# Mixture-of-experts layer on one Trainium2 core: the fourth unit of the shared expert's first row pair by seven products

## The chip, the cores and the metric

The kernel runs on one core of one Trainium2 chip. The metric is the device time of one execution in microseconds (us). Inside the core five engines run their own instruction streams and wait for each other by semaphores: TensorE (PE: matmuls, and PEld: loading their stationary operand), VectorE (DVE), ScalarE (ACT), GpSimd (POOL) and SyncE (SP), whose queue starts the transfers.

## The reference, cut to what matters

```python
# x: (8, 512, 256); gate, up: (256, 1024); down: (1024, 256); 8 experts, top 2 for each of the 8 rows
def _gemma_mlp(x, gate_w, up_w, down_w):
    g = einsum('bsh,hi->bsi', x, gate_w)
    u = einsum('bsh,hi->bsi', x, up_w)
    return einsum('bsi,ih->bsh', gelu(g) * u, down_w)
...
rw = softmax(router_logits); w, sel = top_k(rw, 2)          # weights of the two experts of a row
out = sum over the two experts of w * _gemma_mlp(x, skill_gate[e], skill_up[e], skill_down[e])
out = out + _gemma_mlp(x, shared_gate, shared_up, shared_down)
x = x + out
x = x + (x @ W_base.T + b_base + 2 * sum_e cond_8[e] * (x @ A_e.T) @ B_e.T)
```

## The kernel before, in words

All matmuls are fp32 in three passes. Each operand is split into a rounded part (hi, made on ACT by `take_hi`) and the rest (lo, made on DVE by `take_lo`, L1395, which reads the operand and its hi), and a product is hi x hi, hi x lo, lo x hi: three matmuls of 128x512 (`product`, L733). So nothing can be multiplied before ACT and then DVE have gone over it.

The shared expert comes first. The 8 rows are taken as four pairs (q = 0 to 3), the inner width of 1024 as four pieces of 256 (j = 0 to 3): unit u = 4q + j, 16 units (`NU`). A unit multiplies a 2x2 block matrix of weights (A11, A12, A21, A22; one each for gate and up) with a 2x2 block matrix of tokens (B11, B12, B21, B22). Units of q = 0 do it in the plain way: `outputs(u, GATE)` and `outputs(u, UP)`, four outputs each, two products an output, 24 matmuls. Units of q > 0 do it Strassen-Winograd's way: `matrix(u, part)`, seven products, 21 matmuls. For these, sums of weights (S1 to S4) and of tokens (T1 to T4) are needed: POOL makes them (`left_sums(j)`, four subtractions of 2x128 columns; the T sums at L633 to L647, of 512 columns), ACT and DVE split them (`split_sums`, `split_right`). They are made during q = 0 for q = 1, and the weight sums are kept.

The products land in four PSUM banks (`ring`). In the plain way ACT takes each gate output with GELU (`gelu_block`) and DVE multiplies it with the up output (`mul_block`, L1438, into `post`, semaphore `sh_mul`); ACT and DVE then split the result (`inner_part`), and TensorE multiplies it with the down weights (`shared_down_part`, 12 matmuls at a time). The order on TensorE for each unit is: gate of u, first half of down of u-1, up of u, second half of down of u-1. Output t of the gate of unit u waits until `mul_block` t of unit u-1 has emptied its bank, and output t of the up part until GELU t has emptied it. In `matrix`, products 0 to 3 open the four banks in turn, after three matmuls each in place of six.

Each engine's list is written out by hand, in the order of the program; an instruction that waits holds up all behind it. Around the change lie, for DVE, `turn_x` (STREAM_TRANSPOSE of the next rows' tokens, L1425), `route` (MAX and MAX_INDEX over the logits, L1491 to L1497), `route_weights` (nine small operations, L1502 to L1522), `split_left` (lo of the weights), `split_shared_down` and `split_right`; for ACT, an Exp for the routing (L1210), which needs another activation table than GELU, `take_xt` (copies of the turned tokens of q = 0) and the hi parts of the same splits.

Of the kernel before, what the change touches and what calls it, by code (L numbers as in the profile page):

```python
# [17 lines left out]
GATE, UP = 0, 1  # L18
# [17 lines left out]
def cond_resid_kernel(nc, x, cond, skill_gate, skill_up, skill_down, shared_gate, shared_up,  # L36
# [11 lines left out]
    NU = Q * PAIRS  # L48
    assert HC == 2 and TT == 4 and E * R == P and H == 256 and S == 512 and E == 8
# [15 lines left out]
    with ExitStack() as ctx:  # L65
# [93 lines left out]
        u1, v57 = (post[:, n * S:(n + 1) * S] for n in range(2))  # L159
        g_t = [post[:, (3 + n) * S:(4 + n) * S] for n in range(4)]  # L160
# [182 lines left out]
        t_made = sem("t_made")  # L343
        v_done = sem("v_done")
# [20 lines left out]
        def matrix_no(u, part):  # L365
            return 2 * (u - PAIRS) + part

        def products(u, part, n):
            return 8 * PAIRS + NP * matrix_no(u, part) + n + 1
# [7 lines left out]
        LEFT_SUMS = [5, 7, 9, 10]  # L377
# [21 lines left out]
        def _(sp):  # L399
# [92 lines left out]
            for q in range(Q - 1):  # L492
# [12 lines left out]
                if q == 1:  # L505

                    sp.wait_ge(experts_known, 1)
                    sp.wait_ge(left_ready, LEFT_SUMS[PAIRS - 1])
# [30 lines left out]
            def row(b, first, last):  # L539
                if first:  # L540
# [7 lines left out]
                    sp.wait_ge(c_done, 4 * (NU - PAIRS))  # L548
                    sp.wait_ge(c22_done, 2 * (NU - PAIRS))
# [36 lines left out]
        def _(pool):  # L586
# [6 lines left out]
            def left_sums(j):  # L593
# [4 lines left out]
                s1, s2, s3, s4 = (s_tmp[:, :, n, :] for n in (S1, S2, S3, S4))  # L598
# [10 lines left out]
            left_sums(0)  # L609

# [12 lines left out]
            for u in range(NU):  # L623
                q, j = divmod(u, PAIRS)
                qn = q + 1
                if q > 0:
                    c22(u, GATE)
                if qn < Q and j == 1:
# [11 lines left out]
                if q > 0:  # L640
                    c22(u, UP)
                if qn < Q and j == 1:

                    pool.wait_ge(xt_in, 4 * q + 4)
                    G.tensor_tensor(t_b, xt(1, 1), xt(1, 0), ALU.subtract).then_inc(t_made, 1)
                    pool.wait_ge(t_made, 4 * q + 1)
                    G.tensor_tensor(t_c, xt(1, 1), t_a, ALU.subtract).then_inc(t_made, 1)  # L647
                if u < PAIRS - 1:
# [79 lines left out]
        def _(pe):  # L728
# [63 lines left out]
            def matrix(u, part):  # L792
                q, j = divmod(u, PAIRS)
                m = matrix_no(u, part)
                if part == GATE and q == 1:
                    pe.wait_ge(left_ready, LEFT_SUMS[j])
                for n, (bank, a, b, opens) in enumerate(PRODUCTS):
# [21 lines left out]
                    else:  # L819
                        pe.wait_ge(v_done, m + 1)  # L820
                    product(ring[bank][:], [left(j, hl, part, a) for hl in range(2)],
                            [right(q, hl, b) for hl in range(2)], opens, True, not opens)\
# [36 lines left out]
            for u in range(1, NU):  # L859
                if u < PAIRS:  # L860
# [132 lines left out]
            def row(b, par, first):  # L993
                pe.wait_ge(x_ready, b + 1)
                for k in range(K):
# [20 lines left out]
                    else:  # L1016
                        pe.wait_ge(u1_done, 2 * (NU - PAIRS))
# [5 lines left out]
                    else:  # L1023
                        pe.wait_ge(c_done, 4 * (NU - PAIRS) - 1 + k)
# [35 lines left out]
        def _(act):  # L1060
# [6 lines left out]
            def split_left(j):  # L1067
                act.wait_ge(sh_landed[j], 32)
                take_hi(lefts(j, 0, slice(0, 2), S1, A12 + 1), raw4(j)).then_inc(left_hi, 1)

            def split_sums(j):

                act.wait_ge(s_made, j + 1)
                act.wait_ge(product_done, 8 * (j + 1))
                take_hi(lefts(j, 0, slice(0, 2), S2, S1 + 1), s_tmp).then_inc(left_hi, 1)
# [11 lines left out]
            def split_right(qn, n, src):  # L1087
                if qn > 0 and n == B11:

                    if qn > 1:  # L1090
                        act.wait_ge(product_done, products(PAIRS * (qn - 1) - 1, UP, NP - 1)
                                    if qn > 2 else 8 * PAIRS)
# [34 lines left out]
            def copy_out(u, part):  # L1127

                m = matrix_no(u, part)
                for n, to, bank in ((0, u1, 0), (1, v57, 2)):  # L1130
                    act.wait_ge(product_done, products(u, part, n))
                    if n == 0 and m > 0:

                        act.wait_ge(c_done, 2 * m)
                        act.wait_ge(c22_done, m)
                    nc.scalar.copy(to, ring[bank][:]).then_inc(copied, 1)
# [52 lines left out]
            for u in range(1, NU):  # L1189
# [3 lines left out]
                if q == 0:  # L1193
                    inner_part(u - 1, 2)
                    inner_part(u - 1, 3)
                    for t in range(4):
                        gelu_block(u, t, BANKS[t])
                    if u < PAIRS - 1:
                        split_left(u + 1)
# [8 lines left out]
                if u == 2:  # L1208
# [600 lines left out]
```

## Time and profile before

| | us |
|---|---|
| median of 3 runs | 804.69 (803.77 to 805.49) |
| the profiled execution | 805.0 |
| its span in the profile | 803.2 |
| TensorE busy | 795.5 (99%) |
| VectorE busy | 670.9 (84%) |
| ScalarE busy | 472.1 (59%) |
| GpSimd busy | 271.9 (34%) |

The profile's times count from the start of its span; the execution's own time is 1.8 us longer than the span. An engine is busy while an instruction of it runs; matmuls overlap, so that a busy TensorE says only that it had no gap.

### The profile page before, as it was taken

To read this page: it belongs to the slowest core of one execution; us is meant where nothing else is said; L and a number is where in the kernel's file an instruction comes from. 1 tells how busy PE (TensorE), PEld (TensorE's weight loads), DVE (VectorE), ACT (ScalarE), POOL (GpSimd) and SP (SyncE) were. 2 spreads that over 40 slices of the span, in tenths; PEclk is the share of its full clock that TensorE was granted. 3 is DMA by queue.
4 is the path that set the end of the run, shared out by engine and by line. 5 is a ranking of instruction groups with operands and counts; after the bars stand their busy time and mean duration, and the time that the engine had idled before them with its cause. 6 is when DMAs were issued, how large, how long until landed. Compare 5 with 4: busy or idle time off the path is not lost.

```text
span 803.2 us, 13016 instructions
## 1 busy us (share of the span) xinstructions
PE 795.5 (99%) x4014; PEld 679.7 (85%) x4014; DVE 670.9 (84%) x874; ACT 472.1 (59%) x715; POOL 271.9 (34%) x266
## 2 busy tenths in 40 slices
PE   9999999999999999999999999999999999999998
PEld 7888888888888888889888888888888888888887
DVE  3886987987876799799979879987987997999786
ACT  5574564564654565566556556656665665665563
POOL 1440321321110562443246044333404614423420
PEclk9999999999999999999999999999999999999999
DMA  6340520303213432353443335335244423634200
GB/s 198 86 119 11 147 79 12 120 1 97 100 40 80 159 117 79 105 144 107 137 122 97 104 101 158 111 104 131 89 125 138 122 79 104 161 97 135 66 1 28
DMA packets 120143, 80.56 MB, mean 100 GB/s; under 512 B 62481, under 2 KB 115473, under 8 KB 120081
## 3 DMA queue, kind: packets, MB, share of 16 engines
q1 hardware_dynamic: 120080, 79.88, 33.8%
q8 instruction: 21, 0.34, 0.2%
q14 instruction: 42, 0.34, 0.1%
HBM read 67.28 MB, written 12.58 MB: 99 GB/s over the span
## 4 chain that ended last, share of the span: by engine, by line
PE 91%; DVE 4%; issue 2%; POOL 1%; ACT 1%; DMA 0%; DVEq 0%; POOLq 0%; ACTq 0%
PE ps_ring L733 57%; PE ps_acc L733 33%; DVE inner_lo L1395 1%; DVE wide L1395 1%; DVE xc L1395 1%; PE ps_ring L853 1%; DVE post L1711 0%; DMA sh_scratch<-stage 0%; DVE post L1660 0%; PE ps_acc L941 0%; PE ps_acc L847 0%; ACT xc L1062 0%; DVE post L1651 0%; POOL post L692 0%; ACT wide L1062 0%
## 5 line engine op out<-in xcount | busy, mean ns | idle before, releaser
L733 PE MATMUL ps_ring<-xc,wide 128*128 128x512 f32 (+1 forms) x2076 | 454.9, 367 | 1.8 <-DVE post L1660 1.8
L733 PEld LDWEIGHTS ps_ring<-xc,wide 128*128 128x128 f32 x2076 | 366.1, 188 | 68.6 <-DVE post L1660 2.7
L1062 ACT CAST inner_hi<-post 128x512 fp32r<-128x512 f32 x192 | 117.8, 621 | 131.6 <-DVE post L1711 57.8
L733 PE MATMUL ps_acc<-inner_hi,wide 128*128 128x512 f32 x504 | 172.0, 390 | 0.0
L1395 DVE TENSOR_TENSOR inner_lo<-post,inner_hi 128x512 fp32r<-128x512 f32 x192 | 163.6, 866 | 6.7 <-ACT inner_hi L1062 5.7
L1065 ACT ACTIVATE post<-ps_ring 128x512 f32<-128x512 f32 (+1 forms) x132 | 73.4, 559 | 92.2 <-PE ps_ring L733 86.3
L733 PEld LDWEIGHTS ps_acc<-inner_hi,wide 128*128 128x128 f32 x504 | 94.7, 188 | 19.2
L692 POOL TENSOR_TENSOR post<-post 128x256 f32<-128x256 f32 x48 | 34.5, 740 | 214.6 <-DVE post L1662 214.6
L733 PE MATMUL ps_acc<-inner_lo,wide 128*128 128x512 f32 x252 | 98.3, 390 | 0.0
L1711 DVE SCALAR_TENSOR_TENSOR post<-post,coef_now,ps_ring 128x512 f32<-128x512 f32 x80 | 59.5, 744 | 42.1 <-PE ps_ring L733 39.0
L733 PE MATMUL ps_acc<-inner_hi,sh_dn 128*128 128x512 f32 x256 | 83.8, 389 | 0.0
L733 PE MATMUL ps_ring<-xc 128*128 128x256 f32 x576 | 77.2, 283 | 0.5 <-DVE post L1711 0.5
L621 POOL TENSOR_TENSOR post<-post 128x512 f32<-128x512 f32 x24 | 31.1, 1294 | 135.5 <-DVE post L1447 135.5
L1395 DVE TENSOR_TENSOR wide<-raw,wide 128x1536 fp32r<-128x1536 f32 (+3 forms) x38 | 62.5, 1644 | 15.8 <-ACT wide L1062 15.8
L1065 ACT ACTIVATE post<-post 128x256 f32<-128x256 f32 (+1 forms) x84 | 46.4, 569 | 49.5 <-DVE post L1669 33.6
L733 PEld LDWEIGHTS ps_ring<-xc 128*128 128x128 f32 x576 | 72.6, 192 | 0.7 <-DVE post L1711 0.7
L1395 DVE TENSOR_TENSOR wide<-xbuf,wide 128x1536 fp32r<-128x1536 f32 x32 | 57.4, 1793 | 0.0
L733 PEld LDWEIGHTS ps_acc<-inner_hi,sh_dn 128*128 128x128 f32 x256 | 48.0, 188 | 9.9
L1062 ACT CAST wide<-raw 128x1536 fp32r<-128x1536 f32 (+3 forms) x40 | 52.2, 1306 | 4.8 <-DMA raw<-_L_cond_shared_gate_dram 3.7
L733 PEld LDWEIGHTS ps_acc<-inner_lo,wide 128*128 128x128 f32 x252 | 47.4, 188 | 9.0
L733 PE MATMUL ps_acc<-inner_lo,sh_dn 128*128 128x512 f32 x128 | 49.8, 389 | 0.0
L1395 DVE TENSOR_TENSOR xc<-stage,xc 128x1024 fp32r<-128x1024 f32 (+1 forms) x41 | 47.6, 1166 | 0.0
(122 smaller groups left out, 847.1 us busy)
## 6 DMA issues: line engine op xcount, KB each, us to landing
raw<-n_L_cond_skill_gate_dram SPq DMA_DIRECT2D x32, 256.0 KB, 2.9
raw<-in_L_cond_skill_up_dram SPq DMA_DIRECT2D x32, 256.0 KB, 3.4
raw<-n_L_cond_skill_down_dram SPq DMA_DIRECT2D x32, 256.0 KB, 3.7
xbuf<-n_L_cond_skill_gate_dram SPq DMA_DIRECT2D x32, 256.0 KB, 2.9
xbuf<-in_L_cond_skill_up_dram SPq DMA_DIRECT2D x32, 256.0 KB, 3.4
xbuf<-n_L_cond_skill_down_dram SPq DMA_DIRECT2D x32, 256.0 KB, 4.1
xt_scratch<-xbuf SPq DMA_DIRECT2D x8, 512.0 KB, 3.1
sh_scratch<-stage SPq DMA_DIRECT2D x8, 512.0 KB, 2.7
```

The source lines that it names most:

```text
L621: G.tensor_tensor((g_t if part == GATE else i_t)[3], v57, u1, ALU.add).then_inc(c22_done, 1)
L692: last = G.tensor_tensor(ex_v[:, half], ex_v[:, half], ex_u1[:, half], ALU.add)
L733: last = pe.matmul(dst, left_[a], right_[b], start=start and n == 0, stop=stop and n == len(PASSES) - 1, skip_group_check=adds)
L853: pe.transpose(ring[3][:, 0:P], ident[:], ident[:])
L1062: return nc.scalar.copy(dst, src)
L1065: return nc.scalar.activation(dst, src, ACT.Gelu_apprx_tanh)
L1395: return V.tensor_tensor(dst, src, hi.bitcast(F32), ALU.subtract)
L1711: V.scalar_tensor_tensor(out=inner[k % 2], in0=gelu[k % 2], scalar=coef_now[:, par, s:s + 1], in1=ring[2 + k % 2][:], op0=ALU.mult, op1=AL ...
```

## The change

The fourth unit (u = 3, j = 3 of q = 0) is computed by `matrix` too, 2 x 21 matmuls in place of 2 x 24. What that needs is made earlier:

- the four token sums of q = 0: POOL makes them behind `left_sums(0)`, ACT and DVE split them in the first unit (`split_first`), into buffers of q = 1 and q = 0 that are free then. For POOL to start, ACT copies the turned tokens before `split_left(1)`;
- the weight sums of j = 3: `left_sums(3)` and `split_sums(3)` move into the third unit (u = 2); they were made in the fourth, and split on ACT there and on DVE in the fifth;
- `route` moves on DVE from unit 2 to unit 1, `route_weights` from unit 3 to unit 2, and the Exp on ACT from behind the GELUs of unit 2 to ahead of them;
- T4 of q = 1, whose buffer the first sum uses, is split in unit 3, behind `sums(3, UP)`; `split_shared_down(3)` moves to the end of unit 3 on DVE; the hi part of the weights of j = 3 leaves out A21 (384 columns in place of 512 each for gate and up).

```diff
+    SU = PAIRS - 1
+    NM = NU - SU
...
-        LEFT_SUMS = [5, 7, 9, 10]
+        LEFT_SUMS = [5, 7, 10, 9]
...
             left_sums(0)
+
+            pool.wait_ge(xt0_in, 4)
+            G.tensor_tensor(t0_a, xt(1, 0), xt(0, 0), ALU.subtract).then_inc(t0_made, 1)
+            G.tensor_tensor(t0_b, xt(1, 1), xt(1, 0), ALU.subtract).then_inc(t0_made, 1)
+            pool.wait_ge(t0_made, 1)
+            G.tensor_tensor(t0_c, xt(1, 1), t0_a, ALU.subtract).then_inc(t0_made, 1)
+
+            pool.wait_ge(t0_ready, 1)
+            pool.wait_ge(t0_made, 3)
+            G.tensor_tensor(t0_a, xt(0, 1), t0_c, ALU.subtract).then_inc(t0_made, 1)
...
+                if u == SU - 1:
+
+                    pool.wait_ge(sh_landed[SU], 32)
+                    pool.wait_ge(t0_ready, 4)
+                    left_sums(SU)
...
-                if part == GATE and q == 1:
+                if part == GATE and u < SU + PAIRS:
                     pe.wait_ge(left_ready, LEFT_SUMS[j])
...
+                    if u == SU and part == GATE and n == 1:
+                        pe.wait_ge(t0_ready, 4)
...
             for u in range(1, NU):
-                if u < PAIRS:
+                if u < SU:
                     outputs(u, GATE)
...
+            take_xt(1, acc[0][1])
+            take_xt(2, acc[1][0])
+            take_xt(3, acc[1][1])
             split_left(1)
-            take_xt(1, acc[0][1])
             gelu_block(0, 1, 0)
             split_shared_down(0)
+            split_first(0, FIRST_SUMS[0](0), FIRST_TMP[0])
             gelu_block(0, 3, 2)
-            take_xt(2, acc[1][0])
-            take_xt(3, acc[1][1])
+            split_first(1, FIRST_SUMS[1](0), FIRST_TMP[1])
             inner_part(0, 0)
             inner_part(0, 1)
+            split_first(2, FIRST_SUMS[2](0), FIRST_TMP[2])
             split_sums(0)
+            split_first(3, FIRST_SUMS[3](0), FIRST_TMP[3])
...
+            def split_first(n):
+                dve.wait_ge(t0_hi, n + 1)
+                take_lo(FIRST_SUMS[n](1), FIRST_TMP[n], FIRST_SUMS[n](0)).then_inc(t0_ready, 1)
...
-                if u == 2:
+                if u == 1:
                     route()
-                if u == 3:
-                    route_weights()
...
+                if u == SU - 1:
+                    route_weights()
+                    split_sums(SU)
```

Three places show the moves. First DVE, from the first unit's end up to what stands ahead of the first `mul_block` of unit 1 (`xc<-post` is a `split_first`, `wide<-raw` and `wide<-stage` are weights and weight sums, `inner_lo` is `inner_part`, `post<-post,ps_ring` is `mul_block`). Before:

```order
L1395 TENSOR_TENSOR inner_lo<-post,inner_hi 128x512 x2
L1395 TENSOR_TENSOR wide<-stage,wide 128x2x512
L1395 TENSOR_TENSOR inner_lo<-post,inner_hi 128x512 x2
L1425 STREAM_TRANSPOSE xbuf<-xbuf 128x512 x2
L1425 STREAM_TRANSPOSE xbuf<-stage 128x512 x2
L1395 TENSOR_TENSOR wide<-raw,wide 128x2x512
L1395 TENSOR_TENSOR sh_dn<-raw,sh_dn 128x512
L1395 TENSOR_TENSOR xc<-xbuf,xc 128x512
L1438 TENSOR_TENSOR post<-post,ps_ring 128x512 x2
```

And of the change, the same stretch up to the same weights:

```order
L1455 TENSOR_TENSOR xc<-post,xc 128x512
L1505 TENSOR_TENSOR post<-post,ps_ring 128x512
L1455 TENSOR_TENSOR inner_lo<-post,inner_hi 128x512 x2
L1455 TENSOR_TENSOR xc<-post,xc 128x512
L1455 TENSOR_TENSOR wide<-stage,wide 128x2x512
L1455 TENSOR_TENSOR xc<-post,xc 128x512
L1455 TENSOR_TENSOR inner_lo<-post,inner_hi 128x512 x2
L1492 STREAM_TRANSPOSE xbuf<-xbuf 128x512 x2
L1492 STREAM_TRANSPOSE xbuf<-stage 128x512 x2
L1558 MAX top<-logits 128x8 x8
L1561 TENSOR_TENSOR shifted<-top 128x64
L1564 MAX_INDEX top_e<-top,logits 128x8 x8
```

Three of the four `split_first` (the other is just ahead) and the whole of `route` now stand ahead of unit 1's weights and `mul_block`s.

Second ACT, from the last `inner_part`s of unit 1 through the GELUs of unit 2 (`post<-ps_ring` x4). Before:

```order
L1062 CAST inner_hi<-post 128x512 x2
L1065 ACTIVATE post<-ps_ring 128x512 x4
L1062 CAST wide<-raw 128x2x512
L1062 CAST sh_dn<-raw 128x512
L1210 ACT_TABLE_LOAD
L1210 ACTIVATE expd<-shifted 128x64
L1062 CAST xc<-stage 128x512
```

And of the change:

```order
L1097 CAST inner_hi<-post 128x512 x2
L1251 ACT_TABLE_LOAD
L1251 ACTIVATE expd<-shifted 128x64
L1100 ACT_TABLE_LOAD
L1100 ACTIVATE post<-ps_ring 128x512 x4
L1097 CAST wide<-raw 128x2x384
L1097 CAST sh_dn<-raw 128x512
L1097 CAST xc<-stage 128x512
L1097 CAST wide<-post 128x2x512
```

Two table loads and the Exp now stand ahead of the four GELUs and of the weights of j = 3, and the hi part of the weight sums of j = 3 (`wide<-post`) behind them.

Third DVE, in unit 2, from the token splits to the first two `mul_block`s of unit 2. Before:

```order
L1395 TENSOR_TENSOR wide<-raw,wide 128x2x512
L1395 TENSOR_TENSOR sh_dn<-raw,sh_dn 128x512
L1395 TENSOR_TENSOR xc<-xbuf,xc 128x512
L1395 TENSOR_TENSOR xc<-stage,xc 128x512 x2
L1438 TENSOR_TENSOR post<-post,ps_ring 128x512 x2
```

And of the change:

```order
L1455 TENSOR_TENSOR xc<-stage,xc 128x512 x2
L1569 TENSOR_REDUCE total<-expd 128x8
L1571 RECIPROCAL rtotal<-total 128x8
L1573 TENSOR_TENSOR prob<-expd,rtotal 128x16
L1577 TENSOR_REDUCE psumk<-prob 128x8
L1579 RECIPROCAL rpsumk<-psumk 128x8
L1581 TENSOR_TENSOR wk<-prob,rpsumk 128x16
L1584 TENSOR_SCALAR wk_rest<-wk 128x16
L1586 SCALAR_TENSOR_TENSOR coef<-wk,wk_rest 128x8x2
L1589 TENSOR_SCALAR coef<-lora_w 128x8
L1455 TENSOR_TENSOR wide<-post,wide 128x2x512
L1505 TENSOR_TENSOR post<-post,ps_ring 128x512 x2
```

`route_weights` and the lo part of the weight sums of j = 3 now stand between the token splits and the `mul_block`s of unit 2.

## Rows read from the trace of the kernel before

**Rows 1.** The page, part 1: busy time, share of the span, instructions.

```profile
PE 795.5 (99%) x4014; PEld 679.7 (85%) x4014; DVE 670.9 (84%) x874; ACT 472.1 (59%) x715; POOL 271.9 (34%) x266
```

**Rows 2.** Waits of TensorE over the span: us in total, times, longest.

```profile
PE ps_ring L733 <- DVE post L1660: 1.8, 4, 0.7
```

**Rows 3.** Timeline of TensorE, units 2 to 4: start us, us, instructions.

```profile
35.91 5.64 PE L733 MATMUL ps_ring<-xc,wide 128*128 128x512 f32 x24
...
44.11 5.60 PE L733 MATMUL ps_ring<-xc,wide 128*128 128x512 f32 x24
...
52.27 5.60 PE L733 MATMUL ps_ring<-xc,wide 128*128 128x512 f32 x24
...
68.59 4.92 PE L733 MATMUL ps_ring<-xc,wide 128*128 128x512 f32 x21
```

**Rows 4.** Timeline of DVE ahead of the first `mul_block` of unit 1.

```profile
28.56 1.30 DVE L1425 STREAM_TRANSPOSE xbuf<-stage 128x512 f32<-128x512 f32 x2 [2.71 <-DMA stage<-in_x_dram]
29.79 1.94 DVE L1395 TENSOR_TENSOR wide<-raw,wide 128x1024 fp32r<-128x1024 f32 x1
31.65 1.77 DVE L1395 TENSOR_TENSOR sh_dn<-raw,sh_dn 128x512 fp32r<-128x512 f32 x1
33.34 1.77 DVE L1395 TENSOR_TENSOR xc<-xbuf,xc 128x512 fp32r<-128x512 f32 x1
35.04 1.27 DVE L1438 TENSOR_TENSOR post<-post,ps_ring 128x512 f32<-128x512 f32 x2
```

**Rows 5.** Timeline of POOL: token sums, then weight sums of unit 2.

```profile
29.35 1.29 POOL L633 TENSOR_TENSOR stage<-xbuf 128x512 f32<-128x512 f32 x1 [2.60 <-DVE xbuf L1425]
30.60 2.27 POOL L645 TENSOR_TENSOR stage<-xbuf 128x512 f32<-128x512 f32 x1
32.82 1.75 POOL L647 TENSOR_TENSOR post<-xbuf,stage 128x512 f32<-128x512 f32 x1
...
43.32 0.74 POOL L604 TENSOR_TENSOR stage<-raw,stage 128x256 f32<-128x256 f32 x1
```

**Rows 6.** Timeline of DVE, first unit.

```profile
12.07 1.29 DVE L1395 TENSOR_TENSOR xc<-ps_acc,xc 128x512 fp32r<-128x512 f32 x2 [2.28 <-ACT xc L1062]
...
15.02 1.22 DVE L1395 TENSOR_TENSOR wide<-raw,wide 128x1024 fp32r<-128x1024 f32 x1
```

**Rows 7.** Timeline of ACT: a token copy; then units 1 to 3.

```profile
13.34 0.62 ACT L1085 COPY xbuf<-ps_acc 128x512 f32<-128x512 f32 x1
...
39.90 2.28 ACT L1065 ACTIVATE post<-ps_ring 128x512 f32<-128x512 f32 x4
43.23 1.05 ACT L1062 CAST wide<-raw 128x1024 fp32r<-128x1024 f32 x1 [1.04 <-DMA raw<-in_L_cond_shared_up_dram]
...
44.81 1.28 ACT L1210 ACT_TABLE_LOAD   x1
...
46.27 0.60 ACT L1062 CAST xc<-stage 128x512 fp32r<-128x512 f32 x1
```

**Rows 8.** Timeline of DVE, unit 2 and `route_weights` in unit 3.

```profile
41.88 0.63 DVE L1491 MAX8 top<-logits 128x8 f32<-128x8 f32 x8
...
44.35 1.20 DVE L1395 TENSOR_TENSOR wide<-raw,wide 128x1024 fp32r<-128x1024 f32 x1
45.48 0.68 DVE L1395 TENSOR_TENSOR sh_dn<-raw,sh_dn 128x512 fp32r<-128x512 f32 x1
46.08 0.68 DVE L1395 TENSOR_TENSOR xc<-xbuf,xc 128x512 fp32r<-128x512 f32 x1
...
47.88 1.27 DVE L1438 TENSOR_TENSOR post<-post,ps_ring 128x512 f32<-128x512 f32 x2
...
51.06 0.68 DVE L1438 TENSOR_TENSOR post<-post,ps_ring 128x512 f32<-128x512 f32 x1
...
55.52 0.20 DVE L1502 TENSOR_REDUCE total<-expd 128x8 f32<-128x64 f32 x1
...
57.38 0.16 DVE L1522 TENSOR_SCALAR coef<-lora_w 128x8 f32<-128x8 f32 x1
```

More of the change, by code:

```diff
@@ L159, in cond_resid_kernel @@
         u1, v57 = (post[:, n * S:(n + 1) * S] for n in range(2))
+        t0_a, t0_b, t0_c = (post[:, n * S:(n + 1) * S] for n in range(3))
+        s_tmp3 = post[:, 0:2 * S].rearrange("p (g n c) -> p g n c", g=2, n=4)
         g_t = [post[:, (3 + n) * S:(4 + n) * S] for n in range(4)]
@@ L820, in matrix @@
                         pe.wait_ge(v_done, m + 1)
-                    product(ring[bank][:], [left(j, hl, part, a) for hl in range(2)],
-                            [right(q, hl, b) for hl in range(2)], opens, True, not opens)\
+                    if u == SU and part == GATE and n == 1:
+                        pe.wait_ge(t0_ready, 4)
+                    rights_ = [right(1, hl, T4) if q == 0 and b == T1 else right(q, hl, b) for hl in range(2)]
+                    product(ring[bank][:], [left(j, hl, part, a) for hl in range(2)], rights_, opens, True, not opens)\
                         .then_inc(product_done, 1)
@@ L1068, in split_left, with split_first @@
                 act.wait_ge(sh_landed[j], 32)
-                take_hi(lefts(j, 0, slice(0, 2), S1, A12 + 1), raw4(j)).then_inc(left_hi, 1)
+                if j < SU:
+                    take_hi(lefts(j, 0, slice(0, 2), S1, A12 + 1), raw4(j)).then_inc(left_hi, 1)
+                else:
+                    take_hi(lefts(j, 0, slice(0, 2), A11, A12 + 1), raw4(j)[:, :, 1:4]).then_inc(left_hi, 1)
             def split_sums(j):
-                act.wait_ge(s_made, j + 1)
-                act.wait_ge(product_done, 8 * (j + 1))
-                take_hi(lefts(j, 0, slice(0, 2), S2, S1 + 1), s_tmp).then_inc(left_hi, 1)
+                if j < SU:
+                    act.wait_ge(s_made, POOL_SUMS[j])
+                    act.wait_ge(product_done, 8 * (j + 1))
+                    take_hi(lefts(j, 0, slice(0, 2), S2, S1 + 1), s_tmp).then_inc(left_hi, 1)
+                else:
+                    act.wait_ge(s_made, POOL_SUMS[j])
+                    take_hi(lefts(j, 0, slice(0, 2), S2, S1 + 1), s_tmp3).then_inc(left_hi, 1)
+            def split_first(n, place, src):
+                act.wait_ge(t0_made, n + 1)
+                take_hi(place, src).then_inc(t0_hi, 1)
             def split_shared_down(j):
@@ L1192, in _ @@
                 more = qn < Q
-                if q == 0:
+                if u < SU:
                     inner_part(u - 1, 2)
                     inner_part(u - 1, 3)
+                    if u == 2:
+                        act.wait_ge(routed, 2)
+                        nc.scalar.activation(expd[:], shifted[:], ACT.Exp).then_inc(exp_done, 1)
                     for t in range(4):
                         gelu_block(u, t, BANKS[t])
-                    if u < PAIRS - 1:
-                        split_left(u + 1)
+                    split_left(u + 1)
                     split_shared_down(u)
@@ L1205, in _ @@
                     gelu_sums(u)
-                if u == 2:
-                    act.wait_ge(routed, 2)
-                    nc.scalar.activation(expd[:], shifted[:], ACT.Exp).then_inc(exp_done, 1)
+                if u == SU:
+                    split_shared_down(u)
                 if more and j == 1 and q == 0:
@@ L1215, in _ @@
                     split_right(qn, T3, t_b)
-                if more and j == 3:
+                if more and j == 3 and q > 0:
                     act.wait_ge(t_made, 4 * q + 4)
@@ L1540, in _ @@
             split_shared_down(0)
+            split_first(0)
             mul_block(0, 1, 3)
+            split_first(1)
             mul_block(0, 3, 1)
@@ L1544, in _ @@
             inner_part(0, 1)
+            split_first(2)
             split_sums(0)
+            split_first(3)
             for u in range(1, NU):
```

76 lines of the change are left out of this document (47 added, 29 removed).

## The prediction

> **What bounds the kernel now.** I read the page first: TensorE is busy for 99% of the span [rows 1]. Then its waits: behind the start, the largest entry is 1.8 us, for a DVE line that belongs to the routed experts [rows 2]; in the shared expert's units there is none. So time can be won there only by giving TensorE less to do, and any wait that the change makes is paid in full. Third, the timelines of TensorE [rows 3], to see when it needs each result, and of the engines that deliver. The reader is to see one number there: the `mul_block` that empties the bank for unit 2's gate runs from 35.04 to 35.73 (0.69 us) [rows 4], and TensorE takes up that gate at 35.91 [rows 3]. The margin is 0.18 us.
>
> **What is removed.** A gate or up part of 24 matmuls takes 5.60 us and one of 21 takes 4.92 [rows 3]. Two parts of unit 3 change: 2 x 0.68 = 1.36 us less. That is all the change can win on TensorE, 0.17% of the time.
>
> **What a DVE and a POOL instruction do to each other.** From 29.35 on the two meet [rows 4, 5]. POOL's first subtraction starts at 29.35 and takes 1.29. DVE's weight split, issued at 29.79, takes 1.94 where the same one takes 1.20 elsewhere [rows 8]; POOL's next takes 2.27; DVE's next two take 1.77 each, where 0.68 is usual [rows 8]. The ends fit a strict turn: one works, the other stands, and the one that stood goes next. The cadences alone are 0.60 for a DVE split of 512 columns, 1.13 for one of 1024 [rows 8], 1.25 for POOL's 512 columns [rows 5], and some 0.7 to 0.8 for a piece of `left_sums` (0.74) [rows 5]. I count operations that read PSUM, transposes and MAX as free of the turn; no row given here proves that, and the bounds below cover it.
>
> **First place, unit 1.** DVE gets four `split_first` (4 x 0.60) and `route` ahead of unit 1's `mul_block`s. `route` lasted 2.47 (41.88 to 44.35), some 0.7 of it behind POOL [rows 8], so 1.8 here. Cover is there: DVE waited 2.71 for a transfer before the second pair of transposes [rows 4].
> The walk, each duration from the cadences above: ACT's last token copy needs DVE's fourth split, over at 12.07 + 1.29 = 13.36, and takes 0.62 [rows 6, 7], so POOL starts its first token sum at 14.05 and ends it at 15.3. DVE's weight split, issued at 15.02 [rows 6], then runs to 16.45; POOL's second sum to 17.7; DVE's `sh_dn` split to 18.3; POOL's third to 19.55; the first `split_first` to 20.15; a `mul_block` to 20.8; meanwhile POOL's fourth, to 21.45; the second `split_first` to 22.05; the other `mul_block` to 22.7; two `inner_part` to 23.9, the third `split_first` to 24.5, the weight sums to 25.65, the fourth to 26.25. Now POOL's `left_sums(1)` starts and takes turns with two `inner_part`: 28.85. Four transposes at 0.65: 31.45 (the transfer waited for came at 28.56, so that cover is used up). POOL makes its three sums of 1.25 from 30.85, `route` goes beside them with one turn of waiting, to 34.5. Then weights, `sh_dn` and B11 (1.13 + 0.60 + 0.60) with one more short turn: 37.0. In the kernel before this point is 35.04. It is 1.96 late, the margin covers 0.18, and TensorE stands about **1.8 us** ahead of unit 2's gate. If the turns cost nothing, the same list of work ends some 5 us earlier and TensorE stands 0; if the transposes take turns too, it stands 2.5 to 3.
>
> **Second place, unit 3's gate.** All behind that `mul_block` shifts by 1.96. ACT was free for unit 2's GELUs at 39.90 [rows 7], now 41.86. It loads the Exp table, does the Exp (together 1.46, 44.81 to 46.27), and loads the GELU table (1.28) [rows 7], with gaps 2.76 to 2.8: 44.65. The four GELUs took 2.28 [rows 7]: 46.85. TensorE wants the first at 44.11 + 1.8 = 45.9 [rows 3]; it is there at 45.25, so the loads are hidden at this point. What is late next is behind them: the hi part of j = 3's weights (three quarters of 1.05), ready at 47.65. The transfer was there at 43.23 [rows 7], no bound.
> DVE stands from about 43.85 until then, since that split is next in its list. Then weights (0.87), `sh_dn`, B21, T1 and T3 (4 x 0.60) make 3.27, and the two `left_sums(3)` pieces that POOL has left take turns with them, 1.57: 52.5. `route_weights` is 2.02 (55.52 to 57.54) [rows 8]: 54.5, or 55.15 if its small two-operand steps stand behind POOL's T4. The lo part of the weight sums, 1.15: 55.65 to 56.3. Only then come the `mul_block`s of unit 2, and they took 51.06 + 0.68 - 47.88 = 3.86 from first start to last end [rows 8]. The seven products ask for all four banks, the fourth after three products of 0.68: at 52.27 + 1.8 + 2.04 = 56.1 [rows 3]. It is free at 59.5 to 60.2. So TensorE stands 3.4 to 4.1, I take **3.8 us**, the most of it in one piece ahead of the first product. In the kernel before DVE had begun these `mul_block`s at 47.88 [rows 8], 4.4 us ahead of need; the change puts all its new work into that lead and shortens the need by 3.4 as well.
>
> I find nothing behind: products 4 to 6 of this gate wait for copies and sums that DVE and ACT reach in time (0.1 us over), and the fifth unit gets its weight sums long before. SP's load of j = 3 goes out some 3 us later, still ahead of its use.
>
> **A page's price.** The Trainium skill, page "ScalarE: Activation LUTs", section "What ACT_TABLE_LOAD costs", states about 1283 ns for a load and about 1380 ns of drain with it, 2.66 us for each switch. The load's row agrees with the first number (1.28), and the row of the Exp's successor (46.27 after a load at 44.81) shows no drain. By that page the two switches would end 2.6 us later and so would the time, about 811.5.
>
> **The sum.** -1.36 + 1.8 + 3.8 = +4.2 us. The profiled execution is 805.0 (span 803.2 and 1.8 around it), so it would be 809.2; it stood 0.3 above the median of the three runs, 804.69, and against that I forecast **808.9**. A measurement of this kernel can tell about 0.2%, 1.6 us, from no change.
>
> **The rivals.**
> - *The work is hidden; not slower.* One mechanism: the turns don't add up, DVE finds its way past POOL, and reaches unit 1's `mul_block`s by about 34. Then the GELUs of unit 2 are bound by their products and not by the loads, j = 3's weights are split from 44, and `mul_block` 2 begins near 50.4, the latest start at which the fourth bank is free in time. TensorE stands nowhere: 804.69 - 1.36 = 803.3. It decides at a total wait of 1.36 (equal) and 2.96 (slower by more than 0.2%). For it: 2.71 us of idle in the first unit, and a DVE busy for only 84%. Against: the long durations in [rows 4]. Chance 0.27, waits between 0 and 2.9 included.
> - *Only the second place stands.* Unit 1's extra work fits into its cover, but DVE comes no earlier than before; then the second wait remains at 3.8: 804.69 - 1.36 + 3.8 = 807.1. Chance 0.17.
> - *More than forecast.* Either the swap of tables costs more when a load follows the Exp at once, which no row shows, or TensorE's clock falls after the long stand. The granted clock is full in all 40 slices of the page, with no stand of over 1.5 us; my forecast has one of 2.8. No row shows this kernel at 1.2 GHz; at that level a part of 4.92 us can at most double. Either gives 811 to 814. Chance 0.08.
> - *The shared expert's units gain beyond the removed matmuls*, more than 1.6 in all: no row shows a wait there that could go. Chance 0.03.
> - *Forecast*, both places: 0.45.
>
> **How the numbers follow.** The predicted time is the forecast's, 808.9; its own range is 807.3 to 810.3, from a first wait of 1.2 to 2.5 and a second of 3.2 to 4.3. For 8 in 10 the range reaches from the fully hidden case, 803.3, to 810.6; outside lie the expensive cases and the unexplained gain. Slower by over 0.2%: 0.45 + 0.15 (most of "only the second place") + 0.08 = 0.68; within 0.2%: 0.28; faster: 0.04.
>
> **What would show it.** In the changed kernel's profile: the two parts of unit 3 with 21 matmuls of 4.92 us; TensorE waiting for DVE's `mul_block` (L1505) ahead of unit 2's gate, 1 to 2.5 us, and ahead of unit 3's first four products, 3 to 4 in three pieces; POOL's token sums at 14 us and DVE's splits of 1.2 to 1.9 beside them; DVE idle for over 3 us, released by ACT's `wide`, ahead of the 128x768 split; the first `mul_block` of unit 2 at 55 to 56. I am wrong if DVE gets to unit 1's `mul_block` by 35.2, if the 128x768 split starts before 46, or if another wait appears in units 4 to 16 that the table of waits before did not have.

## The result and the profile after

The changed kernel takes 807.78 us (median of 8 runs, 806.57 to 808.28), the kernel before 804.91 in the same comparison (8 runs, 803.77 to 805.49). The ratio is 1.0035, interval 1.0026 to 1.0044: slower by 2.9 us. The profiled execution took 807.09 us, its span is 805.2.

The waits of TensorE after, in us in total, times and longest. Against [rows 2] the first entry is new; it is the `mul_block` (L1505 now):

```profile
PE ps_ring L765 <- DVE post L1505: 2.9, 4, 1.7
PE ps_ring L765 <- DVE post L1733: 1.6, 3, 0.8
```

The timeline of TensorE after, units 1 to 4. Its columns are those of [rows 3]; the bracket is the idle time ahead and what ended it:

```profile
10.60 13.86 PE L765 MATMUL ps_ring<-xc,wide 128*128 128x512 f32 x60
...
34.95 0.39 PE L765 MATMUL ps_acc<-inner_hi,sh_dn 128*128 128x512 f32 x1
36.11 5.72 PE L765 MATMUL ps_ring<-xc,wide 128*128 128x512 f32 x24 [0.77 <-DVE post L1505]
...
44.39 5.60 PE L765 MATMUL ps_ring<-xc,wide 128*128 128x512 f32 x24
...
52.32 0.39 PE L765 MATMUL ps_acc<-inner_hi,sh_dn 128*128 128x512 f32 x1
54.39 1.62 PE L765 MATMUL ps_ring<-xc,wide 128*128 128x512 f32 x6 [1.68 <-DVE post L1505]
56.27 0.96 PE L765 MATMUL ps_ring<-xc,wide 128*128 128x512 f32 x3 [0.26 <-DVE post L1505]
57.47 3.01 PE L765 MATMUL ps_ring<-xc,wide 128*128 128x512 f32 x12 [0.24 <-DVE post L1505]
...
63.04 4.92 PE L765 MATMUL ps_ring<-xc,wide 128*128 128x512 f32 x21
```

Both predicted waits are there. An idle time understates a wait, since matmuls overlap, so I count from start to start. Ahead of unit 2's gate TensorE loses 36.11 - 34.95 - 0.23 (one matmul) = 0.93 and 0.1 inside the block: 1.0 us. In unit 3's gate 54.39 - 52.32 - 0.23, then 56.27 - 54.39 - 6 x 0.227 and 57.47 - 56.27 - 3 x 0.227: 1.84 + 0.52 + 0.52, and 0.1 in the last block: 3.0 us. Less the 1.36 saved, that is 2.6 to 2.7.

The spans of two profiles start at different places: the block of 60 matmuls of unit 0 begins at 11.30 in the kernel before and at 10.60 here. So I compare stretches. The *front part* runs from that block to a group of 12 matmuls that all kernels have, behind the shared expert, and the *rest* from there to the last six matmuls. Of before:

```profile
11.30 13.89 PE L733 MATMUL ps_ring<-xc,wide 128*128 128x512 f32 x60
...
278.12 1.69 PE L733 MATMUL ps_ring<-xc 128*128 128x256 f32 x12 [0.54 <-DVE post L1711]
...
798.81 0.87 PE L961 MATMUL ps_ring<-xc,sh_dn 128*128 128x256 f32 x6
```

and of after:

```profile
280.05 1.69 PE L765 MATMUL ps_ring<-xc 128*128 128x256 f32 x12 [0.54 <-DVE post L1784]
...
800.82 0.87 PE L996 MATMUL ps_ring<-xc,sh_dn 128*128 128x256 f32 x6
```

The front part was 266.82 and is 269.45, 2.63 longer: the waits less the saving. The rest was 520.69 and is 520.77. Nothing else moved. The 0.70 by which the block of 60 starts earlier is not the change's: it starts between 10.52 (e6) and 11.30 (e1) in kernels whose code ahead of it is the same.

### The profile page after: what moved, and what is told of

Its sections match the earlier page's. It is cut to its first block, busy times and chain, and to the rows that moved or that the text cites. A ratio compares the mean times of both kernels' runs of the same rounds, so it can differ in the third digit from the quotient of the medians.

```text
span 805.2 us, 13039 instructions
## 1 busy us (share of the span) xinstructions
PE 794.3 (99%) x4008; PEld 677.5 (84%) x4008; DVE 678.8 (84%) x886; ACT 476.1 (59%) x723; POOL 278.9 (35%) x272
## 4 chain that ended last, share of the span: by engine, by line
PE 89%; DVE 6%; ACT 2%; issue 2%; DMA 1%; POOL 1%; DVEq 0%; SPq 0%; ACTq 0%; POOLq 0%
PE ps_ring L765 55%; PE ps_acc L765 32%; DVE xc L1455 1%; DVE inner_lo L1455 1%; DVE wide L1455 1%; DMA raw<-_L_cond_shared_gate_dram 1%; DVE post L1505 0%; DMA sh_scratch<-stage 0%; ACT inner_hi L1097 0%; DVE sh_dn L1455 0%; PE ps_acc L976 0%; ACT xc L1097 0%; ACT post L1100 0%; DVE xbuf L1492 0%; DVE post L1733 0%
## 5 line engine op out<-in xcount | busy, mean ns | idle before, releaser
L1100 ACT ACTIVATE post<-ps_ring 128x512 f32<-128x512 f32 (+1 forms) x129 | 71.3, 559 | 86.4 <-PE ps_ring L765 84.9
L724 POOL TENSOR_TENSOR post<-post 128x256 f32<-128x256 f32 x48 | 34.5, 740 | 217.7 <-DVE post L1735 217.7
L646 POOL TENSOR_TENSOR post<-post 128x512 f32<-128x512 f32 x26 | 34.0, 1308 | 140.2 <-DVE post L1514 140.2
L1455 DVE TENSOR_TENSOR wide<-raw,wide 128x1536 fp32r<-128x1536 f32 (+4 forms) x38 | 62.1, 1635 | 19.0 <-ACT wide L1097 19.0
L1100 ACT ACTIVATE post<-post 128x512 f32<-128x512 f32 x87 | 48.2, 571 | 50.5 <-DVE post L1742 33.5
L1097 ACT CAST wide<-raw 128x1536 fp32r<-128x1536 f32 (+4 forms) x40 | 52.0, 1301 | 3.7 <-DMA raw<-_L_cond_shared_gate_dram 3.7
```

The costliest lines, as they stand in the source:

```text
L646: G.tensor_tensor((g_t if part == GATE else i_t)[3], v57, u1, ALU.add).then_inc(c22_done, 1)
L724: last = G.tensor_tensor(ex_v[:, half], ex_v[:, half], ex_u1[:, half], ALU.add)
L1097: return nc.scalar.copy(dst, src)
L1100: return nc.scalar.activation(dst, src, ACT.Gelu_apprx_tanh)
L1455: return V.tensor_tensor(dst, src, hi.bitcast(F32), ALU.subtract)
```

## The experiments

All were timed beside the kernel before, whose medians in the three batches were 804.66, 804.86 and 804.63. "First" and "second" are what TensorE idles ahead of unit 2's gate and within unit 3's gate. Front and rest are against before, each from one profile; two profiles of one program (e4, e13) differ in them by 0.4 and 0.6, so a smaller difference in these two columns is not read by itself.

| kernel | first | second, in pieces | front | rest | median | ratio (interval) |
|---|---|---|---|---|---|---|
| changed | 0.77 | 1.68 + 0.26 + 0.24 | +2.63 | +0.08 | 807.78 | 1.0035 (1.0026 to 1.0044) |
| e1 Exp back | 0.76 | 0.48 + 0.28 + 0.24 | +1.43 | +0.61 | 806.5 | 1.0020 (1.0011 to 1.0029) |
| e2 all three back | 0.59 | 0.15 + 0.26 + 0.23 | +0.96 | +0.82 | 805.97 | 1.0015 (1.0006 to 1.0024) |
| e3 `mul_block`s first, unit 1 | 0 | 1.26 + 0.26 + 0.24 | +1.20 | 0.00 | 806.4 | 1.0021 (1.0012 to 1.0030) |
| e4 no first token sums | 0 | 0.19 + 0.26 + 0.23 | +0.12 | +3.53 | 808.6 | 1.0049 (1.0036 to 1.0063) |
| e5 splits, no sums | 0 | 0.88 + 0.27 + 0.24 | +0.81 | +0.99 | 806.33 | 1.0015 (1.0006 to 1.0024) |
| e6 weights back | 0.78 | 0.48 + 0.28 + 0.23 | +1.44 | -0.41 | 806.28 | 1.0025 (1.0014 to 1.0035) |
| e7 e2 with e3 | 0 | 0.23 | -0.50 | +0.27 | 804.66 | 1.0000 (0.9991 to 1.0009) |
| e9 e7, first in unit 2 too | 0 | 0 | -1.40 | -0.01 | 803.51 | 0.9984 (0.9975 to 0.9993) |
| e10 changed, first in both | 0 | 1.21, later | +0.13 | +1.10 | 805.56 | 1.0006 (0.9997 to 1.0015) |
| e11 routing back | 0.59 | 1.27 + 0.26 + 0.23 | +3.67 | -0.19 | 809.12 | 1.0054 (1.0041 to 1.0067) |
| e12 e9, Exp and routing early | 0 | 0 | -1.42 | -0.54 | 803.86 | 0.9991 (0.9982 to 1.0000) |
| e13 e4 again | 0 | 0.56 + 0.27 + 0.24 | +0.49 | +2.95 | 808.26 | 1.0046 (1.0033 to 1.0059) |

### What stands ahead of the second place

**e1: the Exp behind unit 2's GELUs again.**

```diff
-                    if u == 2:
-                        act.wait_ge(routed, 2)
-                        nc.scalar.activation(expd[:], shifted[:], ACT.Exp).then_inc(exp_done, 1)
                     for t in range(4):
                         gelu_block(u, t, BANKS[t])
...
+                if u == 2:
+                    act.wait_ge(routed, 2)
+                    nc.scalar.activation(expd[:], shifted[:], ACT.Exp).then_inc(exp_done, 1)
```

> The changed kernel with one move undone: the Exp and its two table loads stand behind unit 2's GELUs and weight casts again. Changed kernel: 807.8. Theory (DVE's work in a row ahead of unit 2's mul_blocks, started by ACT's cast of j = 3's weights): the 128x768 split starts at about 43.5 in place of 45.9, but it now meets POOL's left_sums(2) and left_sums(3) and takes turns with them, so that the first mul_block of unit 2 starts only about 1.1 us earlier (52.4): about 806.7. Rival 1 (the table loads alone make the second wait): the whole 2.8 us comes back, 805.0. Rival 2 (the loads are hidden, as they were for the GELUs): no change, 807.8.

As expected, the front part is 1.20 us shorter than the changed kernel's, and the first wait did not move. The Exp's place costs 1.2 us here.

**e6: `route_weights` alone back in the fourth unit.**

> The changed kernel with the routing weights alone put back into the fourth unit. Theory (VectorE's chain ahead of unit 2's mul_blocks loses 2.3 us, but its weight-sum split then meets GpSimd's fourth token sum and stands a turn): the first mul_block of unit 2 comes 1.0 to 1.5 us earlier, the waits ahead of unit 3's gate fall from 3.0 to 1.5 to 2.0 us, the front part lies at +1.1 to +1.7 us against before, the median near 806.6. Rival (the 2.3 us come back whole): waits of 0.7 us or less, front part +0.3, median 805.3.

Also 1.2 us, not the 2.3 that left DVE's list. The weight-sum split now meets POOL's fourth token sum, as expected:

```profile
50.03 2.31 DVE L1455 TENSOR_TENSOR wide<-post,wide 128x1024 fp32r<-128x1024 f32 x1
52.26 1.27 DVE L1505 TENSOR_TENSOR post<-post,ps_ring 128x512 f32<-128x512 f32 x2
...
49.59 1.67 POOL L669 TENSOR_TENSOR stage<-xbuf,post 128x512 f32<-128x512 f32 x1 [1.83 <-DVE xc L1455]
```

In the changed kernel that split takes 1.22, for there the weights' small steps had stood the turn.

**e2: routing, weights and Exp all back.**

> The changed kernel with route in unit 2, route_weights in unit 3 and the Exp behind unit 2's GELUs, as before the change; seven products for unit 3 and its sums stay. Theory: the second wait goes (first mul_block of unit 2 at about 50.2), the first stays at 0.7 to 0.9, since it comes of the four new splits and of POOL's turns and not of route, which lies beside POOL's sums: 807.8 - 3.0 = 804.8. Rival 1 (the first wait is route's 1.96 us): both go, 803.6. Rival 2 (the weight sums of j = 3 on POOL and DVE make the second wait, wherever the routing stands): 806.5 or more.

805.97 came out, between the theory's 804.8 and rival 2's 806.5; the first wait is 0.59. The second is mostly gone (0.15 in its first piece), but unit 2's first `mul_block` comes only 1.7 us earlier than in the changed kernel, counted from the block of 60. POOL's `left_sums(3)` takes turns with DVE to 49.3, ACT's hi part waits for it (first row) and ends just as DVE gets there, and DVE's split then stands behind the fourth token sum (second row):

```profile
49.32 1.06 ACT L1097 CAST wide<-post 128x1024 fp32r<-128x1024 f32 x1 [2.98 <-POOL post L619]
...
50.41 2.27 DVE L1455 TENSOR_TENSOR wide<-post,wide 128x1024 fp32r<-128x1024 f32 x1
52.60 1.27 DVE L1505 TENSOR_TENSOR post<-post,ps_ring 128x512 f32<-128x512 f32 x2
```

### What stands ahead of the first place

**e11: the routing alone back in unit 2**, `if u == 1: route()` made `if u == 2` on DVE.

> The changed kernel with the routing alone put back into unit 2; the exponential stays ahead of unit 2's GELUs and now waits for it. Theory (GpSimd's additions fill the place that the routing leaves, and the exponential starts later): the first wait shrinks by 0.1 to 0.6 us, the GELUs of unit 2 and all behind them come 0.5 to 0.9 us later; the front part lies at +2.6 to +3.1 us against before, the median near 808.0. Rival (the routing's 2 us are the first wait): the first wait is gone, the second stays at 3.0, the front part +1.6, the median near 806.8.

The theory had the direction, not the size of what follows (the GELUs came 1.9 us later, not 0.5 to 0.9). With 2 us less ahead of it, unit 1's first `mul_block` comes only 0.15 us earlier, counted from the block of 60 (35.72 - 11.18 against 35.29 - 10.60). POOL's sums of q = 1 fill the gap: all three splits now stand a turn.

```profile
30.48 1.93 DVE L1455 TENSOR_TENSOR wide<-raw,wide 128x1024 fp32r<-128x1024 f32 x1
32.33 1.77 DVE L1455 TENSOR_TENSOR sh_dn<-raw,sh_dn 128x512 fp32r<-128x512 f32 x1
34.02 1.77 DVE L1455 TENSOR_TENSOR xc<-xbuf,xc 128x512 fp32r<-128x512 f32 x1
35.72 1.27 DVE L1505 TENSOR_TENSOR post<-post,ps_ring 128x512 f32<-128x512 f32 x2
```

And a new wait appears: the Exp waits 2.06 for the routing, the GELUs start at 45.62, and TensorE stands for them at unit 2's up part.

```profile
46.27 5.74 PE L765 MATMUL ps_ring<-xc,wide 128*128 128x512 f32 x24 [1.30 <-ACT post L1100]
```

So the early routing does not cost the changed kernel time; beside the early Exp, which waits for it, it saves 1.0.

**e4: no token sums of the first row pair**, neither made nor split; `matrix(3)` takes plain blocks.

> The changed kernel without the token sums of the first row pair: POOL's four subtractions and the four splits on ACT and DVE are left out, and unit 3's seven products read plain token blocks in their place, so the output differs from the reference. Theory: DVE's list is 2.4 us shorter ahead of unit 1's mul_blocks and POOL's four turns are gone, so that the mul_blocks come 1.5 us earlier; the first wait goes and the second shrinks from 3.0 to 2.3: about 806.1. Rival 1 (route makes the first wait): both waits stay, 807.8. Rival 2 (the first unit's sums are all that is wrong): both go, 803.6.

The first wait is gone, as expected, but the rest of the theory was too cautious: unit 1's first `mul_block` came 2.5 us earlier, not 1.5 (2.2 in e13), and all waits together are 1.5 us (0.12 + 1.36; 1.9 in e13), not 2.3. The median is higher than the changed kernel's, from the rest, which this edit does not touch. I come back to that under e13.

**e5: the splits without the sums**, POOL's four subtractions (the "additions" of the expectation) removed, ACT and DVE splitting plain blocks in their place.

> GpSimd makes no token sums of the first row pair; ScalarE and VectorE still split four blocks there, plain token blocks in place of the sums, so that part of the output is not the reference's. It tells VectorE's longer list from the turns that it takes with GpSimd's additions in 12 to 20 us. Theory (the length of VectorE's list decides; three of the four additions lie beside work that has slack): most of the first wait stays, 0.5 to 1.0 us, the second stays at 3.0, and the front part lies at +1.9 to +2.6 us against before, the median near 807.3. Rival (the turns carry it): VectorE's list is 1.5 us shorter by 24 us, the first wait is gone, the front part lies at +0.8 to +1.5, the median near 806.1.

The theory fell; the rival holds. DVE has the same operations, but those that stood beside POOL at 14 to 21 us (1.48, 1.38, 1.78 and 1.40 in the changed kernel) are short, 2.8 us less together:

```profile
14.54 1.22 DVE L1445 TENSOR_TENSOR wide<-raw,wide 128x1024 fp32r<-128x1024 f32 x1
16.36 0.69 DVE L1445 TENSOR_TENSOR sh_dn<-raw,sh_dn 128x512 fp32r<-128x512 f32 x1 [0.60 <-ACT sh_dn L1087]
16.97 0.69 DVE L1445 TENSOR_TENSOR xc<-xbuf,xc 128x512 fp32r<-128x512 f32 x1
18.01 0.69 DVE L1495 TENSOR_TENSOR post<-post,ps_ring 128x512 f32<-128x512 f32 x1 [0.36 <-PE ps_ring L755]
18.62 0.68 DVE L1445 TENSOR_TENSOR xc<-xbuf,xc 128x512 fp32r<-128x512 f32 x1
```

Unit 1's first `mul_block` comes 1.8 us earlier (33.69 - 10.82 against 35.29 - 10.60), and the first wait is gone. So the four splits alone make no wait; it takes the turns of POOL's subtractions. Whether those would make it without the splits was not run.

**e3: in unit 1 DVE takes the first two `mul_block`s ahead of two splits.**

```diff
                 if u < SU:
                     split_left(u + 1)
-                    split_shared_down(u)
+                    if u != 1:
+                        split_shared_down(u)
...
                     mul_block(u, 1, BANKS[1])
+                    if u == 1:
+                        split_shared_down(u)
+                        split_right(qn, B11, xt(0, 0), rights(qn, 1))
                     inner_part(u, 0)
```

> The changed kernel, with the lo parts of the first down weights of unit 1 (sh_dn) and of B11 behind the first two mul_blocks of unit 1 on DVE. Theory: the first wait (0.9 us ahead of unit 2's gate) goes, but the last mul_block of unit 1, from which ACT's chain to the second wait starts, comes no earlier, since the two splits now stand ahead of it; the second wait grows by the same 0.9: about 807.8, no change. Rival (the two waits add up independently): 806.9.

I had expected that the second wait takes back what the first gives. It shrank too, by 0.4 in its first piece, since POOL's third sum now falls beside `mul_block`s, which read PSUM and stand no turn, and the splits behind them pay none:

```profile
33.69 1.27 DVE L1505 TENSOR_TENSOR post<-post,ps_ring 128x512 f32<-128x512 f32 x2
34.88 0.68 DVE L1455 TENSOR_TENSOR sh_dn<-raw,sh_dn 128x512 fp32r<-128x512 f32 x1
35.49 0.68 DVE L1455 TENSOR_TENSOR xc<-xbuf,xc 128x512 fp32r<-128x512 f32 x1
```

### Is it the work, or its order?

**e7: e2 and e3 together.**

> The routing, its weights and the exponential stand where they stood before, and in unit 1 VectorE's two splits stand behind the first two mul_blocks. Theory (two separate delays, which add): the first wait is gone, the second is that of the weight sums of the fourth unit alone, 0.3 to 0.6 us; the front part lies at -0.9 to -0.5 us against before, the median near 804.2. Rival (what is saved in unit 1 is given back, since GpSimd's weight sums of the fourth unit end no earlier): the second wait grows to 1.5 us, the front part +0.2, the median near 805.2.

The theory's front part was -0.9 to -0.5; measured -0.50, median 804.66. A piece of 0.23 is left, since the splits still stand ahead of unit 2's `mul_block`s.

**e9: in unit 2 as well.** On top of e7, DVE's list for unit 2 is

```python
                elif u == 2:
                    mul_block(u, 0, BANKS[0])
                    mul_block(u, 1, BANKS[1])
                    split_right(qn, B21, xt(0, 1), rights(qn, 2))
                    split_sums(SU)
                    inner_part(u, 0)
                    mul_block(u, 2, BANKS[2])
                    split_right(qn, T1, t_a, rights(qn, 3))
                    inner_part(u, 1)
                    mul_block(u, 3, BANKS[3])
                    split_right(qn, T3, t_b, rights(qn, 4))
                    split_sums(u)
```

> As the one with all back and the mul_blocks first in unit 1; in unit 2 too VectorE takes the two first mul_blocks ahead of the right blocks' splits and of the fourth unit's weight sums, and the splits stand between the later mul_blocks. Theory (the saving is real and only the order of VectorE's list hides it): no wait ahead of unit 2's gate and none over 0.2 us ahead of unit 3's; the front part lies at -1.3 to -1.0 us against before, the median at 803.4 to 803.8, below the kernel before. Rival (the fourth unit's weight sums come too late themselves: GpSimd ends them at 49.3 us and their split stands behind): a wait of 1 us ahead of unit 3's gate, the front part at -0.3, the median near 804.6.

TensorE stands nowhere in these units; unit 3's gate is one block, in the place of the three pieces:

```profile
10.56 13.87 PE L765 MATMUL ps_ring<-xc,wide 128*128 128x512 f32 x60
...
51.47 4.92 PE L765 MATMUL ps_ring<-xc,wide 128*128 128x512 f32 x21
...
275.98 1.69 PE L765 MATMUL ps_ring<-xc 128*128 128x256 f32 x12 [0.53 <-DVE post L1799]
```

The front part is 1.40 shorter than before's, a little beyond the 1.0 to 1.3 expected: the whole saving of 1.36. The median of 803.51 lies below both kernels (ratio 0.9984, interval 0.9975 to 0.9993).

**e12: e9, but routing and Exp as early as in the change.**

> As the one with the mul_blocks first in both units, but with the routing in unit 1 and the exponential ahead of unit 2's GELUs as the change has them, and the routing weights in the fourth unit. Theory (routing and exponential were never the cost, their place in front of an urgent mul_block was): the same as with all back, no waits, the front part at -1.4 to -1.2 us, the median at 803.3 to 803.8. Rival (the table swaps cost what they delay): a wait of 0.3 to 1.3 us ahead of unit 3's gate, the front part at -1.0 to 0, the median at 803.9 to 804.9.

Again no wait, front part -1.42, with `route_weights` in the fourth unit as in e9. DVE idles as long for ACT's split as in the changed kernel, and it costs nothing, since the `mul_block`s now come soon behind it:

```profile
44.21 1.00 DVE L1455 TENSOR_TENSOR wide<-raw,wide 128x768 fp32r<-128x768 f32 x1 [4.01 <-ACT wide L1097]
45.13 1.22 DVE L1455 TENSOR_TENSOR sh_dn<-raw,sh_dn 128x512 fp32r<-128x512 f32 x1
46.27 1.27 DVE L1505 TENSOR_TENSOR post<-post,ps_ring 128x512 f32<-128x512 f32 x2
```

**e10: as e12, but `route_weights` behind the fourth `mul_block` of unit 2.**

> The changed kernel with its routing and exponential where it has them, but with VectorE's mul_blocks first in unit 1 and in unit 2, and the routing weights behind the fourth mul_block of unit 2. Theory (only VectorE's order counts, the early exponential and routing cost nothing once the mul_blocks are first): no wait over 0.2 us; the front part at -1.3 to -0.9, the median at 803.4 to 804.0. Rival (the table swaps ahead of unit 2's GELUs delay the banks): ScalarE gives the GELUs 2.8 us later, TensorE waits 0.5 to 1.5 us in unit 2's second matrix or ahead of unit 3, the front part at -0.4 to +0.4, the median 804.5 to 805.3.

Neither: the GELUs were in time, but the weights now stand ahead of the first sums of unit 3's gate (L1512), which its last product waits for. That is a third place:

```profile
56.37 0.69 DVE L1512 TENSOR_TENSOR post<-ps_ring,post 128x512 f32<-128x512 f32 x1
...
57.11 0.98 PE L765 MATMUL ps_ring<-xc,wide 128*128 128x512 f32 x3 [1.21 <-DVE post L1512]
```

**e13: e4 once more.**

> The kernel without the first row pair's token sums once more (plain blocks in their place, so the output is not the reference's). Its front part was as fast as predicted and its later part 3.5 us slower in one profile. Theory (that belongs to this program, by where its code lies in the instruction stream): the later part is again 3 to 4 us longer than before's, the median again 808.6. Rival (it varies from one execution to the next): the later part within 1 us of before's in this profile, while the median may lie anywhere.

The rest is again 2.95 us longer, the median again above 808: it belongs to that program. The first piece of its second wait came out 0.37 above e4's: DVE had stood 1.39 us for a transfer of x ahead of the second pair of transposes, 1.01 in e4, and all behind it lay that much later.

## Why the prediction was right, and what in it was off

Forecast was slower, 808.9; 807.78 came out. The range of 803.3 to 810.6 is wide and reaches down to a faster kernel, so that lying in it says little by itself. The mechanism is the one forecast: two waits of TensorE for `mul_block`s that DVE reaches late. Both terms were too large, and both lie below their own bounds: 1.0 us against 1.2 to 2.5, and 3.0 against 3.2 to 4.3. The forecast's own range has a slip in its sum: with these bounds it starts at 804.69 - 1.36 + 1.2 + 3.2 = 807.7, not 807.3, and ends at 810.1. With the waits as measured the same sum gives 807.3; that the median still lies in the corrected range, by 0.1, is luck.

- **What is removed, -1.36: right.** The block of 21 takes 4.92, and e9 and e12 show the saving whole (-1.40, -1.42).
- **The turns: right.** POOL's first sums take 1.30, 2.27 and 1.74 with DVE's long splits beside them, and e5 removes them. The assumption that operations reading PSUM stand no turn holds in all timelines above (0.67 to 0.69 beside POOL), and so it does for MAX.
- **First term, +1.8: measured 1.0.** The `mul_block` was forecast at 37.0 and came at 35.29, which is 35.99 on the clock of the kernel before (+0.70, from the two blocks of 60). Of the 1.01 us, 0.87 were there before `route`: the transposes end at 30.58 on that clock and not at 31.45, since the walk gave a little too much to the items up to the last `split_first` (0.37), to the two `inner_part` and their turns (0.31) and to the transposes (0.19). The step "`route` goes beside them with one turn of waiting, to 34.5" is wrong as well, but moves the end by little: `route` took 1.96 (29.88 to 31.84) with no turn to speak of (so that 0.5 of its 2.47 in the kernel before lay behind POOL, not the 0.7 read there), 1.09 less than the 3.05 put in for it, and the `sh_dn` split behind it stood that turn, behind POOL's third sum, so that the three splits took 3.45, not 2.5. From the transposes to the `mul_block` 5.55 were forecast and 5.41 measured:

```profile
29.88 0.59 DVE L1558 MAX8 top<-logits 128x8 f32<-128x8 f32 x8
30.51 0.30 DVE L1561 TENSOR_TENSOR shifted<-top 128x64 f32<-128x64 f32 x1
...
31.84 1.23 DVE L1455 TENSOR_TENSOR wide<-raw,wide 128x1024 fp32r<-128x1024 f32 x1
32.98 1.78 DVE L1455 TENSOR_TENSOR sh_dn<-raw,sh_dn 128x512 fp32r<-128x512 f32 x1
34.69 0.68 DVE L1455 TENSOR_TENSOR xc<-xbuf,xc 128x512 fp32r<-128x512 f32 x1
35.29 1.27 DVE L1505 TENSOR_TENSOR post<-post,ps_ring 128x512 f32<-128x512 f32 x2
```

  And POOL's three sums beside them, the first two undisturbed:

```profile
29.44 1.29 POOL L663 TENSOR_TENSOR stage<-xbuf 128x512 f32<-128x512 f32 x1 [0.47 <-DVE xbuf L1492]
30.69 1.29 POOL L675 TENSOR_TENSOR stage<-xbuf 128x512 f32<-128x512 f32 x1
31.94 2.27 POOL L679 TENSOR_TENSOR post<-xbuf,stage 128x512 f32<-128x512 f32 x1
```

  The word for the routing was wrong too: I counted it as work added ahead of the place, and e11 shows that without it POOL's turns fill the same time.
- **Behind unit 1's `mul_block` the shift is passed on: right.** Forecast from it to the 128x768 split were 10.65 us (37.0 to 47.65); measured are 10.65 (35.29 to 45.94), DVE waiting 3.73 for ACT's `wide`. That it fits to the last digit is luck: the GELUs began 0.2 later after it than forecast, and the four of them took 0.3 less. The loads of the tables were hidden from TensorE (unit 2's up part starts at 44.39 without a wait) and late for the split behind them, as argued.
- **Second term, +3.8: measured 3.0.** From the 128x768 split to the first `mul_block` 8.0 to 8.65 were forecast; it took 7.62 (45.94 to 53.56). The step that failed is "the two `left_sums(3)` pieces that POOL has left take turns with them, 1.57": POOL was done at 47.8, in a piece that cost the `sh_dn` split one turn (1.22), and the weight split stood only the end of the piece before (1.29), so that the chain took 4.17 and not 4.84. `route_weights` took 2.31, with `prob` (0.78) behind POOL's fourth sum as suspected, and the last split 1.14. The forecast that the largest piece would be 2.8 fails with it: 1.68.
- **A delay passed on whole is too simple as a rule of price.** "All behind that `mul_block` shifts" held in the changed kernel, not between the experiments: e1, e6 and e3 each take 1.2 to 1.4 us off the front part, but e6 had taken 2.3 us out of DVE's list for its 1.2, and e11 2.0 us for 0.15 at the `mul_block` and a loss at the end. What an edit is worth depends on which split then meets POOL.
- **The signs.** The forecast's times stand on the clock of the kernel before. There unit 1's `mul_block` is at 35.99 (the limit was 35.2) and the 128x768 split at 46.64 (limit 46); no wait appears in units 4 to 16. So no sign of being wrong came; read off the changed profile without the 0.70, 45.94 would have looked like one. One expected sign did miss: unit 2's first `mul_block` is at 54.26, not at 55 to 56.
- **The drain.** An estimate by the page "ScalarE: Activation LUTs" of the Trainium skill, section "What ACT_TABLE_LOAD costs", has the swaps end some 2.6 us later. The trace disagrees: load, Exp, load and GELU follow each other at 1.29, 0.27 and 1.30 us, in one go.

```profile
40.27 1.28 ACT L1251 ACT_TABLE_LOAD   x1
41.56 0.26 ACT L1251 ACTIVATE expd<-shifted 128x64 f32<-128x64 f32 x1
41.83 1.28 ACT L1100 ACT_TABLE_LOAD   x1
43.13 2.07 ACT L1100 ACTIVATE post<-ps_ring 128x512 f32<-128x512 f32 x4
```

- **The rivals.** "The work is hidden" is what e9 and e12 make true by order alone; its ground, the idle time and the 84% of DVE, was sound for the sum of the work and not for its place. In the changed kernel neither "only the second place" nor "more than forecast" happened: the first wait is there, and the granted clock stayed full (0.999).

Between the 2.63 us of the profile's front part and 2.9 in the medians 0.3 stays unexplained, within what two profiles of one program differ.

## What to carry to other kernels

Before work is moved ahead on an engine with a hand-written list, mark the instructions that another engine waits for, and put the new work behind them, not in front: here the same work cost 2.9 us in one order and gained 1.4 in another. Then look for the next such instruction: in e10 nine small operations behind the last `mul_block` stood ahead of another urgent one, and the gain was lost again. Count the idle time of the helper engine from its next urgent instruction, not over the stage. And where two engines take turns, an item taken from one list may come back as turns in the items that follow; put operations that stand no turn beside the other engine's long ones.

## What the runs showed of the hardware that was not expected

`route` beside POOL's 512-column subtractions paid next to nothing (1.96 us; 0.59 for the eight MAX). It has one two-operand operation, `shifted` (TENSOR_TENSOR), and that began when a subtraction had 0.2 us left: 0.30 in the changed kernel. In the kernel before it stood behind most of one, 0.78 (first row). In the changed kernel `prob`, with 16 columns, stood in the same way behind a subtraction of 1.67 (second row); in e10, with POOL idle, it took 0.17. So it is not its small size that keeps an operation out of the turns.

```profile
42.55 0.78 DVE L1494 TENSOR_TENSOR shifted<-top 128x64 f32<-128x64 f32 x1
...
50.59 0.78 DVE L1573 TENSOR_TENSOR prob<-expd,rtotal 128x16 f32<-128x16 f32 x1
```

The routed rows, whose code no experiment edits, took 2.95 to 3.53 us more in both runs of the kernel without the first token sums. TensorE waits there for DVE twice, near 468 and 605 us, which no other kernel shows, because DVE starts late there, at the turn of a row. The first of them, in e13: DVE idles 4.80 us ahead of its first operation behind the turn, against 1.04 in the kernel before (at 459.50).

```profile
462.82 0.75 DVE L1760 SCALAR_TENSOR_TENSOR post<-post,coef_now,ps_ring 128x512 f32<-128x512 f32 x1 [4.80 <-PE ps_ring L752]
...
467.82 0.49 PE L752 MATMUL ps_acc<-inner_hi,wide 128*128 128x512 f32 x1 [1.91 <-DVE post L1678]
```

Why it belongs to this program stays open. It is a reason to read experiments by the stretch that they edit and not by their time alone: by its median e4 would have spoken for the wrong theory.
